# Attention in one kernel: the products with v and the transposes go ahead of the relative chunk in TensorE's order

## The reference

```python
scores = jnp.einsum('bhid,bhjd->bhij', q, k)
rel = jnp.einsum('bhid,pd->bhip', q, rel_key)
rel_idx = jnp.clip(j - i + p - 1, 0, p - 1)
bias = jnp.take_along_axis(rel, rel_idx, axis=3)          # p = 256
logits = jnp.where(j <= i, (scores + bias) * scale, -jnp.inf)
out = jnp.einsum('bhij,bhjd->bhid', jax.nn.softmax(logits, axis=-1), v)
```

## Time and profile before

| what | value |
|---|---|
| median of 3 runs | 734.02 us (732.74 to 735.74) |
| the profiled execution | 734.27 us, its span 732.5 us |
| mean granted clock of TensorE | 0.949 |
| PE busy | 644.9 us (88%) |
| ACT, DVE busy | 572.3 us (78%), 540.9 us (74%) |
| POOL busy | 245.8 us (34%) |
| one steady unit of the attention stage | 49.3 us |

### The profile page before, as it was taken

One profiled execution on the slowest core, in us unless ns is written; L12 is line 12 of the kernel. 1 busy time (PEld: TensorE's weight loads), 2 busy tenths in 40 slices (PEclk: granted clock), 3 DMA queues, 4 the chain that ended last, 5 costly groups with the idle time before them and its releaser, 6 DMA issues.

```text
span 732.5 us, 18946 instructions
## 1 busy us (share of the span) xinstructions
PE 644.9 (88%) x8066; PEld 468.1 (64%) x8066; DVE 540.9 (74%) x923; ACT 572.3 (78%) x660; POOL 245.8 (34%) x175
## 2 busy tenths in 40 slices
PE   4877869999999999999999999977899898998993
PEld 2333446766766766767667667655687687786682
DVE  5898887687777787887867778756677568588546
ACT  1788688989889889898898798886577768677573
POOL 2100540540812804507219037010361531831801
PEclk9989858999999999999999999988999999999998
DMA  7488433141231421422414215140300000000001
GB/s 230 108 233 246 139 105 73 40 113 52 68 99 34 117 69 39 111 66 68 102 34 102 65 34 134 31 145 1 101 2 1 0 1 1 1 30 0 9 21 60
DMA packets 39176, 52.84 MB, mean 72 GB/s; under 512 B 5656, under 2 KB 29640, under 8 KB 36680
## 3 DMA queue, kind: packets, MB, share of 16 engines
q1 hardware_dynamic: 39088, 51.58, 25.7%
HBM read 39.00 MB, written 11.81 MB: 69 GB/s over the span
## 4 chain that ended last, share of the span: by engine, by line
PE 54%; DVE 13%; ACT 12%; issue 5%; POOL 2%; DVEq 0%; ACTq 0%; POOLq 0%
PE p_o L1127 16%; PE p_s L1102 13%; PE p_z L1801 8%; PE p_z L1804 8%; DVE probs L1228 6%; ACT probs L1345 6%; PE p_s L1036 5%; POOL hid_lo L1722 1%; DVE res L1982 1%; ACT hid_hi L1905 1%; ACT o_acc L1354 1%; DVE hid_lo L2006 1%; ACT even_b L1049 1%; ACT odd_b L1049 1%; PE p_o L1139 1%
## 5 line engine op out<-in xcount | busy, mean ns | idle before, releaser
L1102 PE MATMUL p_s<-q_sb,k_sb 96*128 96x128 bf16 (+1 forms) x1600 | 172.2, 250 | 8.6 <-ACT probs L1345 3.5
L1345 ACT ACTIVATE probs<-p_s 128x1024 f32<-128x1024 f32 x160 | 156.7, 1018 | 18.3 <-DVE p_s L1237 10.6
L1127 PE MATMUL p_o<-probs,v_sb 128*32 128x128 f32 (+1 forms) x3200 | 160.1, 332 | 7.5 <-ACT o_acc L1354 4.4
L1345 ACT ACTIVATE probs<-probs 128x1024 f32<-128x1024 f32 x128 | 133.5, 1055 | 36.2 <-DVE probs L1228 36.0
L1005 POOL TENSOR_SCALAR_AFFINE_SELECT even_b<-even_b 128x2048 f32<-128x2048 f32 x31 | 74.4, 2399 | 256.6 <-ACT even_b L1049 256.6
L1102 PEld LDWEIGHTS p_s<-q_sb,k_sb 96*128 96x128 bf16 x1600 | 113.7, 100 | 68.2 <-issue 29.5
L1228 DVE TENSOR_TENSOR probs<-p_s,even_b 128x1024 f32<-128x1024 f32 x96 | 114.9, 1219 | 16.9 <-PE p_s L1102 16.9
L1127 PEld LDWEIGHTS p_o<-probs,v_sb 128*32 128x32 f32 x3200 | 84.7, 111 | 41.1 <-issue 14.1
L1801 PE MATMUL p_z<-hid_hi,h_hi 128*128 128x512 f32 x256 | 102.2, 399 | 1.7 <-POOL hid_lo L1722 1.7
L1804 PE MATMUL p_z<-hid_lo,h_hi 128*128 128x512 f32 x256 | 100.8, 394 | 0.0
L1036 PE MATMUL p_s<-q_rows,rel_w 72*128 72x64 bf16 x2048 | 83.7, 196 | 17.4 <-DVE probs L1228 8.7
(11 more groups left out here) (184 smaller groups left out, 849.9 us busy)
## 6 DMA issues: line engine op xcount, KB each, us to landing
k_sb<-k_dram SPq DMA_DIRECT2D x48, 192.0 KB
q_sb<-q_dram SPq DMA_DIRECT2D x16, 576.0 KB
q_rows<-qr_dram SPq DMA_DIRECT2D x42, 192.0 KB
q_dram<-q_parts SPq DMA_DIRECT2D x12, 256.0 KB, 5.0
k_dram<-k_parts SPq DMA_DIRECT2D x12, 256.0 KB, 4.8
qr_dram<-q_turned SPq DMA_DIRECT2D x12, 256.0 KB, 3.8
x_all<-in_L_attn_x_dram SPq DMA_DIRECT2D x4, 512.0 KB, 4.4
every<-in_L_ffn_h_w_dram SPq DMA_DIRECT2D x2, 1024.0 KB, 8.7
```

Source lines behind the costliest of these rows:

```text
L1102: last = nc.tensor.matmul(slot[:, c:c + n * BLK], k_sb[hg][:, h * S + j * BLK:h * S + (j + 1) * BLK], ap(q_sb[hg], at, [[HG * S, KROWS], [ ...
L1127: last = nc.tensor.matmul(p_o[32 * h:32 * h + 32, at:at + blocks * BLK], v_sb[hg][:, j, h * 32:(h + 1) * 32], probs[n % PBUFS][:, h, col * ...
L1345: nc.scalar.activation(to, got, ACT.Exp, scale=SCALE).then_inc(t_exp, 1)
```

## The change

In each step of the second stage TensorE now issues `late` (the products with v and the transposes) directly after the scores, and the relative chunk and the prepared work of the feed-forward network after that. The tables, the ring's order and the other engines' programs stay as they are.

```diff
@@ -1181,15 +1181,15 @@
         for u in range(NU):
             for k in range(STEPS):
                 scores(u, k)
+                if u > 0:
+                    late(u - 1, k + STEPS)
+                late(u, k)
                 if k in ODD_AT:
                     relative(pe, "odd", u * FILL + ODD_AT[k])
                 if k in EVEN_AT and u < NU - 1:
                     relative(pe, "even", (u + 1) * FILL + EVEN_AT[k])
                 if ffn_at(u, k) is not None:
                     prepare(ffn_at(u, k))
-                if u > 0:
-                    late(u - 1, k + STEPS)
-                late(u, k)
```

## The result

The changed kernel takes 766.04 us (median of 6 runs, 764.77 to 768.61) against 732.85 us before (6 runs). The ratio is 1.0457, with a 95% interval of 1.0441 to 1.0473: slower by 33.2 us. Forecast were 770 us and 36.2 us more. The profiled execution took 766.62 us with a span of 764.9 us.

A forecast was written before the change was run, and what follows sets the result against it. No engine was saturated; TensorE, busiest, shared a ring of slots with VectorE and ScalarE. Late chunks in four chains (11.0 + 14.6 + 3.2 + 7.4) add 36.2 us to about 734: 770 us, 8-in-10 range 745 to 786.

The forecast's parts named there:

- Term A: Step 1: odd chunk 0 comes late, with VectorE's queue behind it; 1.57 us a unit in units 1 to 7.
- Step 5: Products with v fill TensorE's 1.24 us gap, but the wait for VectorE reappears before later scores; costed at nothing.
- the gap would be worth 1.01 us: Step 5: if VectorE were not in the way, filling TensorE's gap would give -1.01 us a unit.
- Term B: Steps 8, 9, 11: late odd chunks delay ScalarE's exponential of step 9 and VectorE's adds; 1.83 us in 8 units.
- odd(4) "lies inside this": Step 8: the copy of odd chunk 4 is 0.47 us late, counted within the 1.83 us of steps 8, 9, 11.
- Terms C and D: Steps 21 and 26 to 28: late even chunks delay ScalarE's copies; 0.45 and 1.06 us in each of 7 units.
- The last unit's projection: Step 20: starts 1.0 us later, hidden by ScalarE's table load; cost 0, or 0.9 us if the load waits.
- The idle time of TensorE: Whole kernel: idle time was to grow by about 36 us, busy time to stay at about 645 us.
- The sum: All units: the chains of late chunks add 36.2 us, giving 770; chance 0.60, own range 761 to 780.
- My fourth rival: Added waits bring more 1.2 GHz clock: 779 us if once more in six units, 788 if twice; chance 0.05.
- ready work in the gap is a gain: Step 5: the rule's reading, minus 7 x 1.01 us, 727 us; held as the first rival, faster had chance 0.08.

The follow-up runs named there:

- step 1 alone: Kernel before, with the products with v ahead of the relative chunk only at step 1: 742.82 us, ratio 1.0136, period 50.91 us.
- together with step 8: Kernel before, products with v first at steps 5 and 8, copy of odd chunk 2 moved from VectorE to ScalarE: 723.94 us, ratio 0.9877.
- The run with the moved copies: Changed kernel with VectorE's copy of odd chunk 0 and ScalarE's of odd chunk 5 moved behind other work: 757.41 us, ratio 1.0336.
- The run with steps 21 to 28: Kernel before, with the products with v ahead of the chunk only at steps 21, 26, 27 and 28: 742.31 us, ratio 1.0139.
- step 5 alone: Kernel before, with the products with v ahead of the chunk only at step 5: 730.05 us, ratio 0.9967, period 49.31 us.
- step 9 alone: Kernel before, with the products with v ahead of the chunk only at step 9: 737.68 us, ratio 1.0078, period 50.05 us.
- the second run of step 5: Same kernel, products with v first only at step 5, measured again with more rounds: 729.30 us, ratio 0.9952, period 49.31 us.
- ScalarE's copy alone: Kernel before, TensorE's order kept, only the copy of odd chunk 2 moved from VectorE to ScalarE: 733.30 us, ratio 1.0006.
- with the fill: Kernel before, products with v first at step 5, copy of odd chunk 2 moved to ScalarE: 728.36 us, ratio 0.9938, period 48.99 us.
- steps 9 and 11, taken alone: Kernel before, products with v first at only one step: step 9 took 737.68 us (ratio 1.0078), step 11 took 736.17 us (1.0062).

## Why the prediction was right

The direction, the mechanism and the size per unit were right. Point by point:

- Term A, 1.57 us: measured 1.60, by step 1 alone.
- Step 5, nothing: measured 0.00 in the period. The reason was right too: s(6) and s(7) wait for VectorE. The side remark that the gap would be worth 1.01 us without VectorE in the way was too high: it was worth 0.30 us (49.29 to 48.99), and 0.81 together with step 8 (48.48), since odd(4) stood next in line.
- Term B, 1.83 us: measured 1.82. The side remark that odd(4) "lies inside this" was right for the sum, but it is a second path to the exponential of step 9, half as long (about 0.5 us against 1.1). The run with the moved copies found it.
- Terms C and D, 0.45 + 1.06 = 1.51 us: measured 1.57 together. One run holds both; its rows give 0.47 and 1.08.
- The last unit's projection, nothing: confirmed. In the rows of DVE and ACT that answer to the earlier trace rows, the sums are ready after the table load has begun and before it ends:

```profile
520.41 0.17 DVE L133 TENSOR_SCALAR rs<-mv 128x8 f32<-128x8 f32 x1
...
519.70 1.28 ACT L1375 ACT_TABLE_LOAD   x1
520.99 0.21 ACT L1375 ACTIVATE rs<-rs 128x8 f32<-128x8 f32 x1
```

- The idle time of TensorE was to grow by 36 us and its busy time to stay. It is 28 us and 4.4 us, as told above.

The sum was too high by 3.0 us against the 33.2 of the medians, and by 3.8 against the 32.4 by which the profiled execution grew. The ledger of the two profiled executions, by the exponential of step 0 of each unit, shows where. The changed kernel is 0.16 us late at the start of the stage, then:

| stretch | forecast | measured |
|---|---|---|
| unit 0 | 3.3 | 2.7 |
| units 1 to 5 | 24.6 | 25.0 |
| unit 6 | 4.9 | 3.5 |
| unit 7, to the last exponential | 3.4 | 2.0 |
| from there to the end | 0 | -0.9 |

The term that was mis-sized is the clock. The steady units were priced at the full clock, but units 6 and 7 of the kernel before each held a stretch of 3.4 us at 1.2 GHz behind the wait of step 5, about 1.5 us each. The changed kernel has none there. The window of the changed kernel from unit 0 to unit 7:

```profile
113.70:523.10 409.40, 358.23 (x6466) 252.62 (x6464) 290.68 (x313) 326.67 (x341) 137.42 (x71) 1.00 0.27 70
```

My fourth rival had the sign the wrong way round: I let the added waits bring more low clock. They did not. One wait of 1.24 us in a unit was replaced by six of 0.2 to 0.5 us, and even the new wait of 1.04 us ahead of V(4) had no low clock behind it.

Unit 0 is the other part, and it is the clock again. Its start runs at 1.2 GHz, until 11.6 us behind its first exponential in the kernel before and until 10.3 us in the changed kernel. From the exponential of step 0 to that of step 8 they take 14.22 and 13.61 us. The swap at step 5 has no part in these 0.6 us. The run with steps 21 to 28, with the old order there, has the low clock until 10.2 us and also takes 13.61. And step 5 alone (until 9.1 us) takes 13.07, exactly as step 9 alone does with the old order at step 5 (until 9.0 us). The expectation of the second run of step 5 still counted 0.6 us there for the swap. The 0.9 us behind the last unit I did not follow up; nothing of the change lies there.

Why step 5 alone is faster follows from the same. In the two profiled executions of it no stretch of the steady units ran at the low clock (none between 112.9 and 488.4 us in the first), and unit 6 lasted 49.31 us where the kernel before has 50.80. With 1.5 us in unit 6, 1.4 in unit 7 (13.66 us from the exponential of step 0 to that of step 8 before, 12.21 with step 5 alone) that makes 2.9 us, against 2.1 and 3.8 measured. The other executions bear it out: the mean granted clock of the program is 0.9496 over the 17 executions of the kernel before that stand beside the second run, 0.9496 over the 12 with ScalarE's copy alone, which keeps the wait and is no faster, and 0.9532 and 0.9545 over those of step 5 alone (5 and 6).

The rule of the Trainium skill (Perfetto Trace Analysis, Optimization Strategy), to find the gaps of the most contended engine and what blocks them, picks the right gap. But my prediction read into it that ready work in the gap is a gain, and the page does not say so: it asks that the dependency start sooner or complete faster. Here the fill alone was worth 0.00 us a unit. Moving the copy that holds up s(7) was worth 0.02 alone, 0.32 with the fill, and 0.83 with step 8 too. The dependency of the gap itself, the add of step 4, no run made faster; the gap is 1.24 us with the copy moved as well.

## What to carry to other kernels

When two pieces of work on one engine change places, look at who consumes the one that moves back and what stands behind that consumer in its own queue. In a ring of buffers a consumer's wait that ends on exactly this piece is no cover. At step 1 a chunk that came 1.6 us late cost 1.60 us a unit; at steps 9 and 11, taken alone, 0.75 of 1.1 and 1.2 us got through. Before you fill a gap on the busiest engine, look whether another engine's work is due right behind it; here moving one copy to an engine with a matching wait, and two of the nine swaps, gave 1.2%, while all nine swaps cost 4.6%. And compare the period of a steady unit, not only the total: parts measured that way added up to within 0.01 us.

## What the runs showed of the hardware

In the steady units the low clock came only behind the 1.24 us wait ahead of odd(3), and more idle time did not bring it. In the window from 120 to 480 us TensorE is busy 339.5 of 360 us in the kernel before, and the granted clock fell to 0.50 twice, in units 6 and 7, each time within 1.1 us of the end of that wait. In the changed kernel it is busy 316.7 of 360 us and the clock stayed at 1.00. Of the seven profiled kernels that keep the 1.24 us wait, four had such stretches (before 2, step 1 alone 2, steps 21 to 28 1, ScalarE's copy alone 2) and three had none, which makes 7 stretches behind 49 such waits. All six profiled executions in which that wait is broken up had none between unit 1 and the middle of unit 7. So the wait goes with the low clock but does not bring it each time; that it is the cause is the best reading of these executions and not shown by itself. Here is one of the stretches, with ScalarE's copy alone:

```profile
259.40:262.80 3.40, 3.35 (x38) 2.00 (x39) 1.12 (x1) 2.84 (x4) 0.00 (x0) 0.50 0.11 33
```

What decides in which units the clock falls stays open.

A table load on ScalarE starts before what its activation waits for is ready: it began at 519.70, VectorE's value was done at 520.58, and the activation ran at 520.99. The load took 1.28 us, and from the end of the exponential ahead of it (519.68) to the activation it was 1.31 us.
